# First attention's q and k as plain float32 on four groups of 32 rows, in place of high and low parts on two groups of 64

## The reference, cut to what matters

```python
xq = (x @ wq.T).reshape(B, S, 16, 16)      # B = 4, S = 2048; xk and xv likewise
q, k = _apply_rope(xq, cos, sin), _apply_rope(xk, cos, sin)
scores = jnp.einsum('bqhd,bkhd->bhqk', q, k) / jnp.sqrt(16)
attn = jax.nn.softmax(scores, axis=-1)
out = jnp.einsum('bhqk,bkhd->bqhd', attn, xv)
```

## Time and profile before

| what | before |
|---|---|
| time, median of 3 runs | 5153.57 us |
| span of the profiled execution | 5142.3 us (its runs' median is 11.3 us above it: what lies around the span) |
| mean granted TensorE clock | 0.941 |
| TensorE busy | 4714.6 us |
| VectorE busy | 4237.0 us |
| ScalarE busy | 3449.7 us |
| GpSimd busy | 1333.4 us |
| first attention, first matmul to last values | 1260.8 us to 3928 us |

### The profile page before, as it was taken

One profiled execution on the slowest core, in us unless ns is written; L12 is line 12 of the kernel. 1 busy time (PEld: TensorE's weight loads), 2 busy tenths in 40 slices (PEclk: granted clock), 3 DMA queues, 4 the chain that ended last, 5 costly groups with the idle time before them and its releaser, 6 DMA issues. The chain is left out here.

```text
span 5142.3 us, 90411 instructions
## 1 busy us (share of the span) xinstructions
PE 4714.6 (92%) x34043; PEld 2092.5 (41%) x34043; DVE 4237.0 (82%) x5517; ACT 3449.7 (67%) x6176; POOL 1333.4 (26%) x881
## 2 busy tenths in 40 slices
PE   6999786797999999999999999999998879999993
PEld 3444452364333333333333333333334445555542
DVE  6999650397899999999999999999993877777736
ACT  4787310132688888888888888888886326666663
POOL 2233220164000000000000000000001229999992
PEclk9999897898899999999999999999998669999996
DMA  5110479688333333343333344333322941222305
GB/s 182 52 53 33 155 247 385 251 280 232 45 53 48 48 48 48 54 54 51 48 48 48 50 54 53 50 48 48 49 34 76 313 128 42 71 70 67 78 10 167
DMA packets 390773, 498.42 MB, mean 97 GB/s; under 512 B 165440, under 2 KB 278880, under 8 KB 373312
## 3 DMA queue, kind: packets, MB, share of 16 engines
q1 hardware_dynamic: 372448, 465.90, 38.7%
q10 hardware_dynamic: 17888, 26.74, 1.5%
HBM read 325.15 MB, written 165.02 MB: 95 GB/s over the span
## 5 line engine op out<-in xcount | busy, mean ns | idle before, releaser
L792 DVE TENSOR_REDUCE at_NM<-at_MX 128x1 f32<-128x1024 f32 (+1 forms) x3008 | 3085.0, 1050 | 299.5 <-PE at_MX L614 270.9
L734 ACT ACTIVATE at_PB<-at_S 128x512 f32<-128x512 f32 x5056 | 2719.4, 597 | 585.9 <-PE at_S L643 466.0
L614 PE MATMUL at_MX<-at_KT,at_QT 48*128 48x512 f32 (+1 forms) x5056 | 1919.7, 455 | 60.2 <-DMA at_VS<-v 45.6
L643 PE MATMUL at_S<-at_QT,at_KT 50*128 50x512 f32 (+1 forms) x5056 | 1899.9, 441 | 6.0 <-ACT at_PB L734 5.8
L655 PE MATMUL at_AV<-at_PB,at_VS 128*32 128x256 f32 (+1 forms) x18304 | 1567.7, 414 | 16.7 <-ACT at_AVS L742 15.7
L643 PEld LDWEIGHTS at_S<-at_QT,at_KT 50*128 50x128 f32 (+1 forms) x5056 | 801.8, 187 | 876.6 <-ACT at_PB L734 772.0
L614 PEld LDWEIGHTS at_MX<-at_KT,at_QT 48*128 48x128 f32 (+1 forms) x5056 | 791.6, 190 | 311.0 <-DVE at_NM L792 217.7
L655 PEld LDWEIGHTS at_AV<-at_PB,at_VS 128*32 128x32 f32 x18304 | 364.6, 108 | 858.6 <-ACT at_PB L734 745.4
L548 POOL CAST at_NMR<-at_NMF 16x128 fp32r<-16x128 f32 x79 | 22.1, 280 | 1625.3 <-ACT at_NMF L747 1625.3
L575 POOL TENSOR_TENSOR at_SUM<-at_SUM,at_PB 128x2048 f32<-128x2048 f32 x90 | 415.4, 4615 | 10.9
L932 PE MATMUL wkv_PQ<-wkv_XT,wkv_WT 128*128 128x512 f32 x768 | 339.6, 600 | 42.5 <-DVE wkv_DL L1052 25.9
(11 more groups left out here) (209 smaller groups left out, 3531.4 us busy)
## 6 DMA issues: line engine op xcount, KB each, us to landing
moe_W<-in_w SPq DMA_DIRECT2D x64, 1024.0 KB, 11.9
at_QT<-qk SPq DMA_DIRECT2D x402, 128.0 KB, 5.2
at_KT<-qk SPq DMA_DIRECT2D x384, 128.0 KB, 6.6
qk<-r_HI SPq DMA_DIRECT2D x52, 512.0 KB, 5.0
qk<-r_LO SPq DMA_DIRECT2D x52, 512.0 KB, 5.3
at_VS<-v SPq DMA_DIRECT2D x96, 256.0 KB, 9.2
at_KT<-qk SPq DMA_DIRECT2D x96, 256.0 KB, 6.2
ycat<-wkv_Y SPq DMA_DIRECT2D x32, 512.0 KB, 2.6
```

The source lines that it names most:

```text
L614: ins = nc.tensor.matmul(MX[r][:, a, :], q_of(s)[h:h + NQ, b * P:(b + 1) * P], k_of(it, s, b * P // W)[h:h + NQ, (c + a) * W:(c + a + 1) * W],
L643: nc.tensor.matmul(SP_[item(it, s, "score", t)[1]][:, :], k_of(it, s, c)[h:h + NQ + 2, kb * P:(kb + 1) * P], q_of(s)[h:h + NQ + 2, c * W:( ...
L734: nc.scalar.activation(PB[:, t % NPB, :], SP_[r][:, :], ACT.Exp, scale=scale).then_inc(exp_done, 1)
L792: nc.vector.tensor_reduce(NM4[:, b, c:c + 1], MX[r][:, :, :].rearrange("p a n -> p (a n)"), AX_X, ALU.max, negate=True).then_inc(ring_got, 1)
```

## The change

For the first attention `TWO` is now `DH + 1 <= 32`. q and k are held as plain float32 in 16 rows, and the maximum in one row more, at rows 0, 32, 64 and 96 (`COPIES`). Scores take rows 96 and 0 in turn (17 rows), the pair of maxima rows 32 and 64 (16 rows). `phase_rope` stores `QF` itself, without a split, and `qk1` has no parts. The copy of maxima `NMF` goes by two DMAs straight into rows 16 and 112 of `QT`. `set_ones` writes each `KT` tile in one memset of 128 partitions in place of two of 32. The second attention is as it was.

```diff
-    NQ = 3 * DH
-    TWO = NQ + 2 <= 64
-    HALVES = (0, 64) if TWO else (0,)
+    TWO = DH + 1 <= 32
+    NQ = DH if TWO else 3 * DH
+    NS = NQ + 1 if TWO else NQ + 2
+    DT = F32 if TWO else F32R
+    COPIES = (0, 32, 64, 96) if TWO else (0,)
+    SCORE_ROWS = (0, 96) if TWO else (0,)
+    MAX_ROWS = (32, 64) if TWO else (0,)
...
-        QT = [m.sb(f"QT{u}", [P, T], F32R) for u in range(NQB)]
-        KT = [m.sb(f"KT{u}", [P, T], F32R) for u in range(NKB)]
+        QT = [m.sb(f"QT{u}", [P, T], DT) for u in range(NQB)]
+        KT = [m.sb(f"KT{u}", [P, T], DT) for u in range(NKB)]
...
-            for h in HALVES:
-                lo = (h + NQ) // 32 * 32
-                ins = eng.memset(KT[u][lo:lo + 32, :].bitcast(F32), 1.0)
-            return ins
+            lo, hi = (0, P) if TWO else (NQ, NQ + 32)
+            return eng.memset(KT[u][lo:hi, :].bitcast(F32), 1.0)
...
-                for h in HALVES:
-                    for k, part in enumerate((0, 0, 1)):
-                        if it > 0:
-                            sp.dma_start(QT[u][h + k * DH:h + (k + 1) * DH, :].bitcast(F32),
-                                         group(qk_d[0, part], it)).then_inc(loaded[u], 16)
-                    for k, part in enumerate((0, 1, 0)):
-                        sp.dma_start(KT[u][h + k * DH:h + (k + 1) * DH, :].bitcast(F32),
-                                     group(qk_d[1, part], it)).then_inc(loaded[u], 16)
+                for h in COPIES:
+                    if it > 0:
+                        sp.dma_start(QT[u][h:h + DH, :], group(qk_d[0], it)).then_inc(loaded[u], 16)
+                    sp.dma_start(KT[u][h:h + DH, :], group(qk_d[1], it)).then_inc(loaded[u], 16)
...
+                if TWO:
+                    wait(sp, nmf_got, it + 1, sp_step)
+                    for h in SCORE_ROWS:
+                        row = h + NQ
+                        sp.dma_start(q_of(s)[row:row + 1, :], NMF[:, :]).then_inc(mrow, 16)
+                    return
...
-                    h = 64 * a
+                    h = MAX_ROWS[a]
                     ins = nc.tensor.matmul(MX[r][:, a, :], q_of(s)[h:h + NQ, b * P:(b + 1) * P],
...
-                h = HALVES[t % len(HALVES)]
+                h = SCORE_ROWS[t % len(SCORE_ROWS)]
...
-                                 k_of(it, s, c)[h:h + NQ + 2, kb * P:(kb + 1) * P],
-                                 q_of(s)[h:h + NQ + 2, c * W:(c + 1) * W], start=True, stop=True).then_inc(s_put, 1)
+                                 k_of(it, s, c)[h:h + NS, kb * P:(kb + 1) * P],
+                                 q_of(s)[h:h + NS, c * W:(c + 1) * W], start=True, stop=True).then_inc(s_put, 1)
...
-            def split(g, k):
...
             def take_qk(g, k):
                 wait(act, qk_put, 4 * g + k + 1)
-                wait(act, split_done, 4 * g + k - 1)
-                nc.scalar.activation(QF[k % 2][:, :], PQ[:, :], ACT.Copy).then_inc(qk_got, 1)
+                if k == 0:
+                    wait(act, l_st[g % 2], 48 * (g // 2))
+                nc.scalar.activation(QF[g % 2][:, k, :], PQ[:, :], ACT.Copy).then_inc(qk_got, 1)
```

More of the change, by code:

```diff
@@ L273, in phase_attention @@
     NCH = T // W
-    NQ = 3 * DH
-    TWO = NQ + 2 <= 64
-    HALVES = (0, 64) if TWO else (0,)
+    TWO = DH + 1 <= 32
[5 more added lines that the diff above has]
+    MAX_ROWS = (32, 64) if TWO else (0,)
+    Q_PARTS = ((0, 0),) if TWO else ((0, 0), (1, 0), (2, 1))
+    K_PARTS = ((0, 0),) if TWO else ((0, 0), (1, 1), (2, 0))
     VW = 32
@@ L379, in phase_attention @@
         else:
+            NMR = m.sb("NMR", [NBLK, 2, P], F32R)
             ONES = m.sb("ONES", [P, VW])
@@ L450, in load_queries @@
             u = it % NQB
-            for k, part in enumerate((0, 0, 1)):
+            for k, part in Q_PARTS:
                 eng.dma_start(QT[u][k * DH:(k + 1) * DH, c * W:(c + count) * W].bitcast(F32),
@@ L465, in load_lanes @@
                         k_at = KSLOT[bh]
-                        for k, part in enumerate((0, 1, 0)):
+                        for k, part in K_PARTS:
                             sp.dma_start(KT[k_at][k * DH:(k + 1) * DH, :].bitcast(F32),
@@ L475, in load @@
                 wait(sp, av_done, NBLK * (it - 3), sp_step)
[L476 to L483 removed]
+                for h in COPIES:
+                    if it > 0:
+                        sp.dma_start(QT[u][h:h + DH, :], group(qk_d[0], it)).then_inc(loaded[u], 16)
+                    sp.dma_start(KT[u][h:h + DH, :], group(qk_d[1], it)).then_inc(loaded[u], 16)
                 sp.dma_start(VS[u][:, :, :], group(v_d, it)).then_inc(loaded[u], 16)
             def m_row(it, s):
[L488 to L493 removed]
+                if TWO:
[4 more added lines that the diff above has]
+                    return
+                wait(sp, nmr_ready, it + 1, sp_step)
+                for a in range(2):
+                    row = NQ + a
+                    sp.dma_start(q_of(s)[row:row + 1, :].bitcast(F32),
+                                 NMR[:, a, :].bitcast(F32)).then_inc(mrow, 16)
             def store(it, s):
@@ L544, in m_parts @@
             def m_parts(it):
-                wait(pool, mrow, 32 * len(HALVES) * it)
+                wait(pool, mrow, 32 * it)
                 wait(pool, nmf_got, it + 1, pool_step)
@@ L575, in add @@
                 nc.gpsimd.tensor_tensor(total[:, :, :], other, PB[:, k:k + NCH, :], ALU.add).then_inc(sum_done, 1)
-            m_parts(0)
+            if not TWO:
+                m_parts(0)
             def adds(n, s, t):
@@ L590, in window @@
                         normalise_turned(n - 1, s + NBUF - 1)
-                    if t == TURN_AT and later(n, 1):
+                    if not TWO and t == TURN_AT and later(n, 1):
                         m_parts(n + 1)
@@ L718, in _ @@
             if TWO:
[L719 to L722, removed]
+                for h in COPIES:
+                    act.dma_start(QT[0][h:h + DH, :], group(qk_d[0], 0)).then_inc(loaded[0], 16)
             else:
@@ L744, in take_turned @@
             def take_turned(it, i, r):
-                wait(act, nmr_ready, it)
+                if TWO:
+                    wait(act, mrow, 32 * it)
+                else:
+                    wait(act, nmr_ready, it)
                 wait(act, s_put, i + 1)
@@ L1685, in phase_rope @@
         QR = [m.sb(f"QR{u}", [P, J, 2 * D]) for u in range(2)]
-        QF = [m.sb(f"QF{u}", [P, GT]) for u in range(2)]
-        HI = [m.sb(f"HI{u}", [P, 4, GT], F32R) for u in range(2)]
-        LO = [m.sb(f"LO{u}", [P, 4, GT], F32R) for u in range(2)]
+        QF = [m.sb(f"QF{u}", [P, 4, GT]) for u in range(2)]
         VB = [m.sb(f"VB{u}", [P, H, J, VW]) for u in range(2)]
@@ L1700, in phase_rope @@
             "half_turned"))
[L1701 to L1702 removed]
+        proj, vproj, crossed, direct, roped, v_done, qk_put, qk_got = (m.sem(n) for n in (
+            "proj", "vproj", "crossed", "direct", "roped", "v_done", "qk_put", "qk_got"))
         a_ld, x_ld, x_st = ([m.sem(f"{n}{u}") for u in range(NX)] for n in ("a_ld", "x_ld", "x_st"))
@@ L1728, in store_qkv @@
                 sp.dma_start(out[:, :, e * J:(e + 1) * J, :], VB[u][:, :, :, :]).then_inc(l_st[u], 16)
-                qk = qk_d.rearrange("a l (b h) d t -> b a l (h d) t", b=B)[b]
+                qk = qk_d.rearrange("a (b h) d t -> b a (h d) t", b=B)[b]
                 for a in range(2):
[L1731 to L1735, removed]
+                    wait(sp, qk_got, 4 * g + 2 * a + 2)
+                    out = qk[a].rearrange("(c p) t -> p c t", p=P)
+                    sp.dma_start(out[:, :, e * GT:(e + 1) * GT],
+                                 QF[u][:, 2 * a:2 * a + 2, :]).then_inc(l_st[u], 16)
             sp.dma_start(O[:, :, :], eo_d.rearrange("b e d -> e b d")).then_inc(o_ld, 16)
@@ L1781, in scale1 @@
                 nc.gpsimd.tensor_tensor(RS1[g % 2][:, :], VE1[:, :], nhalf[:, :], ALU.pow).then_inc(rs1, 1)
-            def split(g, k):
[L1784 to L1794, removed]
-            for g in range(NGR):
[L1796 to L1807, removed]
+            for g in range(NGR):
+                scale0(g)
+                scale1(g)
         @block.tensor
@@ L1906, in values @@
                 wait(act, rs1, g + 1)
-                wait(act, l_st[u], 80 * (g // 2))
+                wait(act, l_st[u], 48 * (g // 2))
                 for jj in range(2):
```

9 lines of the change are left out of this document (4 added, 5 removed).

## The result

The changed kernel takes 8848.11 us (median of 4 runs, 8847.0 to 8851.62) against 5153.54 us before (4 runs, 5146.32 to 5154.35): 1.718 times as long, with an interval of 1.715 to 1.720. I forecast slower, 6267 us, within 5970 to 6800. The direction was right and the size was not: +3695 us where I had +1113.

A forecast was written before the change was run, and what follows sets the result against it. TensorE was taken to bound the first attention's repeat, VectorE 0.015 us behind. Span 5142.3 + 1096 (repeats) + 27 (stretch before item 0) - 10 (removed work) = 6255, plus 11.3 around it: 6267 us, range 5970 to 6800.

The forecast's parts named there:

- TensorE is the bound before, VectorE right behind: First attention's repeat before the change: TensorE sets 1.24 us, VectorE could go at 1.225, so 0.015 behind.
- The rival of one pass: First attention: float32 on 16 or 17 rows costs as float32r, VectorE's 1.225 sets the repeat; 5113 us, chance 0.05.
- Two passes at twice the length: Scores and maxima: each float32 matmul runs as two passes, each twice as long, 4 times float32r's array time.
- Four groups at once without contention: Scores and maxima: all four matmuls run together as two passes, group 1.08 us; with held scores chance 0.67.
- rivals of contention: Four row groups hinder each other: factor 1.25 on passes, repeat 1.985 us, 6700 us, chance 0.13.
- passes one after another: Matmuls start strictly in order, only neighbours overlap: repeat 2.93 us, about 8630 us; chance 0.13 shared with factor 2.
- The even score held by an exponential: First attention: even score waits for an earlier odd score's exponential, starting 0.125 us late; repeat 1.775 instead of 1.65.
- a clock that falls or anything else 0.02: Leftover case in the list of chances, given 0.02, without a size of its own.
- 2048 x (1.775 - 1.24) = +1096: First attention: 2048 repeats each grow from 1.24 to 1.775 us, adding 1096 us.
- the repeat of 1.65: First attention: TensorE's own repeat, group 1.08 plus values 0.57 us, with the even score not held.
- The stretch ahead of item 0: 43 pairs of maxima before item 0 at clock 0.50 take longer: +27 us, 0 if the clock rises.
- the 3 us more: Inside the rope phase: copies that waited for a split give back perhaps 3 us, part of the -10.

The follow-up runs named there:

- e4: Changed kernel with QT and KT of the first attention as float32r, single passes on 16 and 17 rows; 5109.02 and 5202.77 us.
- e5: Changed kernel with QT and KT as float32r and all four score and maxima matmuls widened to 32 rows; 4937.19 us, ratio to before 0.959.
- e1: Changed kernel, still plain float32, with all four score and maxima matmuls widened to 32 rows; 6196.05 us, ratio to before 1.203.
- e7: Changed kernel with only the two maxima matmuls widened to 32 rows, scores kept at 17; 6257.15 us.
- e6: Changed kernel with 24 dense float32 matmuls of 128 rows added right ahead of score 0 of item 0; 8874.18 us.
- e8: e4 with 24 dense matmuls added ahead of score 0 of item 0; six runs from 4951.01 to 5223.73 us.

## Why the prediction was right or wrong

- **TensorE is the bound before, VectorE right behind.** The first half held. The second failed: I read 1.225 from two neighbouring reductions as VectorE's limit. Ahead of item 0 the same reductions stood 1.13 apart, as I wrote myself, and in e4 and e5 they go at 1.13 to 1.14 beside all the rest. The rival of one pass, priced by 1.225 at 5113 us, comes with 1.138 to 5153.6 + 2048 x (1.138 - 1.24) - 10 = 4935 us at the full clock. Its kernel is e4, and there the clock took it to 5109 and 5203.
- **Two passes at twice the length.** Right: 8192 records, and 0.54 between passes in e1.
- **Four groups at once without contention.** Right. In e1 the group takes 1.18 with the late score in it, against 1.205 reckoned. The rivals of contention and of passes one after another are out: first passes of all four start within 0.02 of each other in the changed kernel, and so do second ones. What the Trainium skill states for four row tiles ("TensorE: Matmul & The Clock Gate", Part 3, 3.07 times one) would by my estimate have made the repeat 2.03 at full clock; 1.75 was measured in e1.
- **The even score held by an exponential.** Right in e1: 0.13 late. At the half clock it doesn't happen: the even score starts 0.02 after the odd one.
- **The step that failed** is the clock: the chance "a clock that falls or anything else 0.02", and behind it the term "2048 x (1.775 - 1.24) = +1096". I summed the repeat with full-clock durations because the first attention ran at 1.00, and never asked whether the new mix would have that clock. That clock was read where the old work stood. The runs showed 0.50 in its place, a repeat of 3.03 and not 1.775, and the same four matmuls at 32 rows brought 1.00 and 1.75 back (e1). The clock is worth 8848 - 6196 = 2652 us between the two. The rows to price it were there: the earlier trace rows has 0.50 for the stretch of maxima alone, 96 rows at two thirds of the time. They didn't say that a TensorE that never pauses could stay there. Twice the repeat of 1.65 is 3.3, from which 5142 + 2048 x (3.3 - 1.24) + 11, about 9370 us, follows as a bound from above. The case had a mechanism, a place and a price, and got neither its own paragraph nor a fair chance.
- **The stretch ahead of item 0**, at 0.50 as reckoned. From the first maxima to the first score it takes 1311.5 - 1260.8 = 50.8 us before, and 1328.3 - 1252.6 = 75.8 in the changed kernel: 25 more, where I had 27.
- **What is removed.** QF's last copy ends at 1236.78 instead of 1237.35, and the first maxima start at 1252.56 where they started at 1260.77. From the one to the other it takes 15.8 us in place of 23.4: -7.6 for the end of the phase and the loads (I had 6.7 for these). Inside the rope phase hardly any of the 3 us more came: ScalarE's copies waited 49.6 us for TensorE and 17.8 for splits before, and wait 69.4 for TensorE now.

The changed kernel's loads and rope end, for comparison with the earlier trace rows:

```profile
1236.18 0.60 ACT L1884 ACTIVATE r_QF<-r_PQ 128x512 f32<-128x512 f32 x1 [0.75 <-PE r_PQ L1838]
...
1243.01 3.35 SPq L483 DMA_DIRECT2D at_KT<-qk  x4
...
1252.53 0.32 SPq L482 DMA_DIRECT2D at_QT<-qk  x1
...
1252.56 3.78 PE L620 MATMUL at_MX<-at_KT,at_QT 16*128 16x512 f32 x8 [16.41 <-DMA at_VS<-v]
```

## What to carry to other kernels

A duration of TensorE is a number of cycles and a clock. When a change narrows its matmuls to fewer rows, price the new repeat at both clocks and give the lower one a real chance; here a TensorE without a gap was no protection from it. Where the work is narrow, rows added to no effect cost no time that shows (e7 and e1 have the same item, 56.89, and the reductions go at 1.138 in e5 as in e4's stretch at 1.00) and can bring the clock back: here they were worth 2652 us on plain float32. And count passes before groups: here four groups in place of two give back a factor of two at best, and float32 in place of float32r costs a factor of four.

## What the runs showed of the hardware that I had not expected

- With 66 rows in use in float32 the granted clock stood at 0.50 for 6 ms while TensorE was busy without a gap, and fell back to it from 1.00 some 5 us after the added matmuls ended (e6). With 98 (e7) or 128 (e1) it was 1.00. The count alone doesn't tell it: two scores of 32 rows beside the values held 1.00 (e1's last item), two of 17 lost it (e7's).
- The added rows count though they add nothing to any result. They hold zeros in `QT` and ones in `KT`, so the zeros are in the moving operand of the scores and in the stationary one of the maxima.
- With 66 rows in single passes (e4, e8) both levels lasted for hundreds of us in one execution: 870 us at 0.50, then 1877 us at 1.00 (e4).
- Reductions of 1024 columns that last 1.21 to 1.23 us by their records follow each other every 1.13 to 1.14 us (e4): the length of a record is not the pace.
